# The last head of an attention kernel: score matmuls in pairs on both halves of the partitions, exponentials of 1024 columns

## The chip, the cores and the metric

One core of a Trainium2 chip runs the whole program. The metric is the device time of one execution in microseconds, as the median of several runs. Before the change it is 1465.34 us (three runs, 1463.74 to 1465.86).

## What is computed

Two sequences of 2048 tokens, width 256: 16-head attention with 16 columns a head and rotary positions, added to the input and normalised; then a gated feed-forward (token shift, sigmoid gate, squared relu key, value) over the same 4096 tokens, added and normalised.

```python
q, k, v = (heads(x @ W + b) for W, b in ((Wq, bq), (Wk, bk), (Wv, bv)))
q, k = rotary(q), rotary(k)
y = layernorm(x + softmax(q @ k.T / sqrt(16)) @ v)
xr = mu_r * y + (1 - mu_r) * y_prev          # y_prev: the token before
xk = mu_k * y + (1 - mu_k) * y_prev
r = sigmoid(xr @ W_r.T)
out = layernorm(y + r * (square(relu(xk @ W_k.T)) @ W_v.T))
```

## The kernel before, in words

The 32 heads (2 sequences x 16) run one after the other. `SEQ` is 2048, `TOK` 512, `P` 128; a head has `TILES` = 16 key tiles of 128 keys and `BLOCKS` = 4 blocks of 512 queries, so 64 items, numbered through all heads by `item(h, kt, j)`. `LAST` is head 31.

Queries and keys of a head lie as a stack of 48 rows (high and low parts, so that a product of rounded floats keeps its accuracy) in `q_stack` and `k_stack`. Two more query rows (against rows of ones in `k_stack`) carry the negative maximum of each query, so that a score matmul of 50 rows gives scores with the maximum already taken off. The stack of head h lies on partitions 0 to 63 if h is even, on 64 to 127 if it is odd (`stack_rows`), in one of two slots (`slot_of`). `load_neg` writes the two rows of maxima, by way of DRAM.

Per head and key tile (`period`, line 716) TensorE does: four score matmuls (line 733), each keys x 512 queries into one of three `score_ps` banks in turn; between them two maximum units for a later head (`maximum`, line 647), each two matmuls of 512 columns into one of two `ring_ps` buffers of two banks; and the value products of the tile before (`pv_half`, line 679), two times four matmuls of 256 columns, each on its own 32 columns of the array, adding into `pv_ps`. The maximum matmuls of a later head stand on the other 64 partitions than the scores: for its first `EARLY` = 8 units such a head reads a copy of its stack that `load_copy` has laid on the other side (512 queries and all the keys).

ScalarE turns every score bank into `probs` by an exponential of 512 columns (line 917). It waits for `scores_ready`, and at the start of a tile for `pv_done`, since `probs` holds two tiles. TensorE waits for `exps_done` before it writes a score bank again and before a value product. VectorE reads each ring buffer with a maximum over 1024 columns (line 1254); after a head it turns `pv_ps` over (`turn_context`), takes the inverse of the sums (`invert_sums`), and POOL scales the context and adds it to the input (`add_context`). TensorE's value products of the next head wait for `pv_turned`.

In the last head no maxima are left. TensorE fills their place with the gate products of the feed-forward's blocks 0 and 1 (`first_r`, `project_r`, line 697) in groups of four matmuls, into the ring buffers. VectorE does the second stage's preparation meanwhile: `before_tokens` and `mix` (the token shift) of block 0, then the context of head 30, then `before_tokens` and `mix` of block 1, then statistics (`tile_stats`), `normalise` and `flip_block` of blocks 2 and 3, whose turned tiles SP lays down by DMA (`land`, 16 DMAs a block), and `before_tokens`, `mix` of block 2. It then waits for the context of head 31.

After the last head TensorE goes through the eight blocks of the feed-forward: `project_key(0)`, then for each n the gate products of block n + 2, `value(n)`, `project_key(n + 1)`. The bank lists `key_ps`, `value_ps` and `r_ps` (ring 0, ring 1, ring 0, ...) say where they go. ScalarE takes the sigmoids of blocks 0 and 1 first, then the key of block 0 (`take_key`), and so on; it has to load another activation table between the exponentials and the sigmoids. Each engine's order is the program's order; the engines meet only at semaphores.

Of the kernel before, what the change touches and what calls it, by code (L numbers as in the profile page):

```python
# [53 lines left out]
EARLY = 2 * LEAD  # L54
COPY_Q = EARLY // 2 * P
FIRST_COPY = SIDES
TWINS = {0: (STACKS - 1, EARLY, MAX_UNITS), 1: (STACKS - 2, 0, EARLY)}
NEG_CYCLE = TILES - LEAD
NEG_LOADS = 1
CTX_BUFS = 2  # L60
R_AHEAD = 2
FLIPS = 4 * 4
POOL_BLOCKS = 2
RECIP_CYCLE = 4
# [98 lines left out]
def build(nc, x_tok, x_blk, w_first, w_qk, b_qk, w_v, b_v, w_rkv, mu, tables, out):  # L163
# [7 lines left out]
    with ExitStack() as ctx:  # L171
# [90 lines left out]
        y_blk = [y_half[:, n] for y_half in (y_first, y_second) for n in range(BLOCKS)]  # L262


        score_ps = [pb(f"score_ps{i}", [P, TOK]) for i in range(SCORE_BANKS)]
        ring_ps = [pb(f"ring_ps{i}", [P, 2 * TOK]) for i in range(2)]
        pv_ps = pb("pv_ps", [P, TOK])
        proj_ps = (*score_ps, pv_ps)
        ring_halves = [ring[:, c * TOK:(c + 1) * TOK] for ring in ring_ps for c in range(2)]
# [41 lines left out]
        copy_in = [sem(f"copy_in{i}") for i in range(SIDES)]  # L311
        ones_set = sem("ones_set")
        neg_in = [sem(f"neg_in{i}") for i in range(STACKS)]
        scores_ready = sem("scores_ready")
        exps_done = sem("exps_done")
        pv_done = sem("pv_done")
# [56 lines left out]
        def stack_rows(h, first, count):  # L373

            side = h % SIDES * SIDE_ROWS
            return slice(side + first, side + first + count)

        def slot_of(h):
            return h // SIDES % (STACKS // SIDES)
# [17 lines left out]
        def _(sp):  # L397
# [24 lines left out]
            def load_copy(h):  # L422

                slot, side, row = slot_of(h + 1), h // QUAD % 2, h % QUAD * HEAD_DIM
                q = cuts[row:row + HEAD_DIM, side, :, 0:COPY_Q]
                k = cuts[QUAD_ROWS + row:QUAD_ROWS + row + HEAD_DIM, side, :, :]
                first = 0
                for a, reps in BAND_GROUPS:
                    rows = stack_rows(h + 1, first * HEAD_DIM, reps * HEAD_DIM)
                    first += reps  # L430
                    sp.dma_start(q_stack[rows, slot, 0:COPY_Q].bitcast(F32), q[:, a:a + 1, :].broadcast_to([HEAD_DIM, reps, COPY_Q]))\
                        .then_inc(copy_in[h % SIDES], DMA)
                    sp.dma_start(k_stack[rows, slot, :].bitcast(F32), k[:, 0:reps, :]).then_inc(copy_in[h % SIDES], DMA)

# [22 lines left out]
            def load_neg(h):  # L457

                sp.wait_ge(neg_flipped, h + 1)
                sp.dma_start(neg_d[h % 2], neg_turned[:, h % 2]).then_inc(neg_out, DMA)  # L460
                sp.wait_ge(neg_out, (h + 1) * DMA)
                dst = q_stack[stack_rows(h, ROWS, PARTS), slot_of(h), :].bitcast(F32)
                sp.dma_start(dst.rearrange("a (t i q) -> a t i q", i=P // VCOLS, q=VCOLS),
                             neg_d[h % 2].rearrange("(i a t) q -> a t i q", i=P // VCOLS, a=PARTS))\
                    .then_inc(neg_in[h % STACKS], DMA)

            sp.dma_start(w_qk_s[:, :, 0:P], w_first).then_inc(w_first_in, DMA)
            for c, signal in enumerate((x_first_in, x_in[0])):
# [121 lines left out]
        def _(pe):  # L590
# [88 lines left out]
            def pv_half(h, kt, half):  # L679
# [8 lines left out]
                if half == 1:  # L688
                    mm.then_inc(pv_done, 1)

            def pv(h, kt):

                for half in range(2):
                    pv_half(h, kt, half)
# [15 lines left out]
                            mm.then_inc(r_ready, 1)  # L710
                        yield

            first_r = itertools.chain.from_iterable(project_r(n, VCOLS) for n in range(R_AHEAD))


            def period(h):

                k = RING_BASE[h]

                pe.wait_ge(neg_in[h % STACKS], neg_loaded(h))  # L720
                for kt, ops in enumerate(period_ops(h)):

                    work = ring_ops(ops, k)
                    k += ring_len(ops)
                    for j in range(BLOCKS):
                        n = item(h, kt, j)
                        rows, slot = stack_rows(h, 0, ROWS_M), slot_of(h)
                        queries = q_stack[rows, slot, :].rearrange("r (c j t) -> r j c t", j=BLOCKS, t=VCOLS)

                        if n < SCORE_BANKS:  # L730
                            pe.wait_ge(evacuated, LAST_IN_BANK[n] - BLOCKS + 1)
                        pe.wait_ge(exps_done, n + 1)
                        mm = pe.matmul(score_ps[n % SCORE_BANKS][:, :], k_stack[rows, slot, kt * P:(kt + 1) * P],  # L733
                                       queries[:, j], start=True, stop=True)
                        mm.then_inc(scores_ready, 1)
                        next(work, None)
                        if j % 2:
                            pv_before(h, kt, j // 2)
                            if h == LAST and kt > 0 and (j > 1 or kt == 1):
                                if (kt, j) == (1, 1):  # L740
                                    pe.wait_ge(ring_freed, RING_CREDIT + RING_TOTAL)
                                next(first_r, None)
                    for _ in work:
                        pass
                if h == LAST:
                    for _ in first_r:
                        pass

            def pv_before(h, kt, half):
# [34 lines left out]
                        next(terms)  # L784
                    done = due
            assert next(terms, None) is None
            for h in range(ALL_HEADS):
                if h == LAST:
                    pe.wait_ge(c_in, 2 * DMA)
                period(h)  # L790
            pv(LAST, TILES - 1)


            def value(n):
# [36 lines left out]
                    mm.then_inc(kv_ready, 1)  # L831

            project_key(0)
            for n in range(END - 2):
                for _ in project_r(n + R_AHEAD, P):
                    pass
                value(n)
                project_key(n + 1)
# [9 lines left out]
        def _(act):  # L848
# [60 lines left out]
            def period(h):  # L909
                for kt in range(TILES):  # L910
                    act.wait_ge(pv_done, h * TILES + kt + 1)
                    for j in range(BLOCKS):
                        if (h, kt, j) == (0, 0, 2):
                            take(len(WORK) - 1)
                        n = item(h, kt, j)
                        act.wait_ge(scores_ready, n + 1)
                        act.activation(probs[:, kt % 2, j, :], score_ps[n % SCORE_BANKS][:, :], ACT.Exp,  # L917
                                       scale=SCALE).then_inc(exps_done, 1)

            for h in range(ALL_HEADS):  # L920
                period(h)


            def take_turned(n):
# [40 lines left out]

            act.wait_ge(c_small, 1)
            act.wait_ge(ones_set, 2)
            for n in range(R_AHEAD):
                sigmoid(n)
            take_key(0)  # L970
            for n in range(A_GROUPS - 1):
                if BLOCKS <= n + R_AHEAD + 1 < A_GROUPS:
                    take_turned(n + R_AHEAD + 1)
# [188 lines left out]
        def _(dve):  # L1162
# [243 lines left out]
            edge(0)  # L1406
            before_tokens(0)
            mix(0)
            turn_context(LAST - 1)
            invert_sums(LAST - 1)  # L1410
            before_tokens(1)
            mix(1)
            tile_stats(range(POOL_BLOCKS * TPB, TILES))
            for n in range(POOL_BLOCKS, BLOCKS):
                normalise(n)
# [117 lines left out]
```

## Time and profile before

| | |
|---|---|
| median of three runs | 1465.34 us |
| profiled execution, its time | 1466.05 us |
| its span | 1464.2 us |
| TensorE busy, share of the span | 1443.7 us, 99% |
| VectorE busy | 1375.7 us, 94% |
| ScalarE busy | 1194.1 us, 82% |
| POOL busy | 307.0 us, 21% |
| first score of the last head | 1334.34 us |
| last value product of the last head ends | 1381.92 us |
| TensorE ends | 1456.2 us |

Times inside the execution count from the start of its span. Busy time of matmuls is modelled, since they are pipelined: two that overlap are each shown with their full length. The chain of waits is followed back from the last instruction, and gives each stretch of time to one piece of work. One float32 product of the program shows as two matmul records.

### The profile page before, as it was taken

How to read it: one execution, taken by the hardware profiler on the slowest of the kernel's cores; microseconds unless marked ns; L12 is line 12 of the kernel's file. 1: busy time of each engine (PE TensorE's matmuls, PEld its weight loads, DVE VectorE, ACT ScalarE, POOL GpSimd, SP SyncE). 2: the span in 40 equal slices, each digit the busy share in tenths (PEclk: the TensorE clock that was granted, in tenths of full speed). 3: DMA queues.
4: the chain of work that ended last, by engine and by line, in shares of the span. 5: the costliest groups of instructions: out<-in, count | busy, mean ns of one | idle time of the engine just before them, and what ended most of it. 6: DMA issues, size and time to landing. Idle time of an engine off the chain costs nothing.

```text
span 1464.2 us, 31722 instructions
## 1 busy us (share of the span) xinstructions
PE 1443.7 (99%) x13128; PEld 603.9 (41%) x13128; DVE 1375.7 (94%) x1459; ACT 1194.1 (82%) x2185; POOL 307.0 (21%) x277
## 2 busy tenths in 40 slices
PE   8999999999999999999999999999999999999998
PEld 6663333333333333333333333333333333333475
DVE  5779999999999999999999999999999999997396
ACT  4448888888888888888888888888888888888745
POOL 3430221032103210022103210331002000001175
PEclk9999999999999999999999999999999999999999
DMA  7755122232223221312223222322111323200153
GB/s 228 229 135 176 28 33 37 36 94 38 37 37 95 37 36 25 82 28 37 37 36 95 37 38 37 95 38 32 25 25 32 52 36 52 37 2 9 24 112 119
DMA packets 73056, 88.50 MB, mean 60 GB/s; under 512 B 48656, under 2 KB 58512, under 8 KB 66704
## 3 DMA queue, kind: packets, MB, share of 16 engines
q1 hardware_dynamic: 72352, 85.69, 27.9%
q8 instruction: 103, 1.69, 0.5%
q10 hardware_dynamic: 560, 0.79, 0.2%
q14 instruction: 41, 0.34, 0.1%
HBM read 29.50 MB, written 14.16 MB: 30 GB/s over the span
## 4 chain that ended last, share of the span: by engine, by line
PE 96%; ACT 1%; DMA 1%; DVE 1%; issue 0%; POOL 0%; POOLq 0%; ACTq 0%; DVEq 0%
PE pv_ps L685 40%; PE score_ps L733 33%; PE ring_ps L666 14%; PE score_ps L623 2%; PE ring_ps L705 2%; PE score_ps L818 2%; ACT probs L917 1%; PE score_ps L639 1%; PE pv_ps L623 1%; PE pv_ps L802 1%; PE score_ps L802 1%; DMA rope<-tables 1%; PE pv_ps L639 0%; PE ring_ps L818 0%; DMA w_raw<-w_first 0%
## 5 line engine op out<-in xcount | busy, mean ns | idle before, releaser
L1254 DVE TENSOR_REDUCE tile_max<-ring_ps 128x1 f32<-128x1024 f32 x1024 | 1232.7, 1217 | 33.7 <-PE ring_ps L666 25.5
L917 ACT ACTIVATE probs<-score_ps 128x512 f32<-128x512 f32 x2048 | 1107.7, 595 | 170.4 <-PE score_ps L733 129.9
L733 PE MATMUL score_ps<-q_stack,k_stack 50*128 50x512 f32 x2048 | 754.9, 448 | 7.1 <-ACT probs L917 6.9
L666 PE MATMUL ring_ps<-k_stack,q_stack 48*128 48x512 f32 x2048 | 733.3, 443 | 0.0
L685 PE MATMUL pv_ps<-probs,v_aug 128*32 128x256 f32 x8192 | 649.0, 391 | 0.0
L733 PEld LDWEIGHTS score_ps<-q_stack,k_stack 50*128 50x128 f32 x2048 | 304.4, 185 | 429.1 <-ACT probs L917 412.2
L685 PEld LDWEIGHTS pv_ps<-probs,v_aug 128*32 128x32 f32 x8192 | 166.0, 108 | 367.3 <-issue 190.0
L666 PEld LDWEIGHTS ring_ps<-k_stack,q_stack 48*128 48x128 f32 x2048 | 299.9, 184 | 7.0 <-DVE tile_max L1254 3.3
L1014 POOL TENSOR_TENSOR neg_cuts<-neg_max,zeros 128x16 fp32r<-128x16 f32 x31 | 6.8, 219 | 496.0 <-DVE neg_max L1227 496.0
L1006 POOL TENSOR_TENSOR v_aug<-v_all,b_v_s 128x256 f32<-128x256 f32 x32 | 23.5, 737 | 312.8 <-PE pv_ps L685 252.9
L1023 POOL TENSOR_TENSOR ctx_part<-ctx_turn,recip 128x256 f32<-128x256 f32 x32 | 20.1, 628 | 268.8 <-DVE recip L1281 268.8
L1035 POOL TENSOR_TENSOR rope<-rope 128x2048 f32<-128x2048 f32 x14 | 63.8, 4573 | 8.6 <-DMA rope<-qk_raw 8.6
L1276 DVE STREAM_TRANSPOSE ctx_turn<-pv_ps 128x512 f32<-128x512 f32 x32 | 22.6, 706 | 22.1 <-PE pv_ps L685 22.1
L868 ACT ACTIVATE probs<-score_ps,b_qk_s 128x512 f32<-128x512 f32 x21 | 14.4, 687 | 24.1 <-PE score_ps L623 24.1
L1041 POOL TENSOR_TENSOR rope<-rope 128x2048 f32<-128x2048 f32 x7 | 32.1, 4582 | 0.1
L1057 POOL TENSOR_TENSOR rope<-rope 128x2048 fp32r<-128x2048 f32 x7 | 32.0, 4570 | 0.1
L705 PE MATMUL ring_ps<-w_rkv_s,rope 128*32 128x256 f32 (+1 forms) x224 | 31.6, 379 | 0.0
L948 ACT ACTIVATE v_all<-score_ps 128x512 f32<-128x512 f32 x14 | 7.6, 594 | 22.7 <-PE score_ps L818 22.7
L705 PEld LDWEIGHTS ring_ps<-w_rkv_s,rope 128*32 128x32 f32 (+1 forms) x224 | 22.5, 144 | 7.3 <-issue 2.4
L818 PE MATMUL score_ps<-rope,w_rkv_s 128*128 128x512 f32 x56 | 25.3, 594 | 0.0
L1356 DVE SCALAR_TENSOR_TENSOR rope<-rope,mu_s 128x512 f32<-128x512 f32 x32 | 22.3, 756 | 2.1 <-ACT rope L929 2.1
L1028 POOL TENSOR_TENSOR z_s<-z_s,ctx_part 128x256 f32<-128x256 f32 x32 | 23.6, 738 | 2.5
(138 smaller groups left out, 546.4 us busy)
## 6 DMA issues: line engine op xcount, KB each, us to landing
k_stack<-rope SPq DMA_DIRECT2D x61, 256.0 KB, 5.2
k_stack<-rope SPq DMA_DIRECT2D x63, 128.0 KB, 4.8
q_stack<-rope SPq DMA_DIRECT2D x31, 256.0 KB, 4.4
qk_raw<-probs SPq DMA_DIRECT2D x28, 256.0 KB, 3.2
rope<-qk_raw SPq DMA_DIRECT2D x7, 1024.0 KB, 4.9
rope<-qk_raw SPq DMA_DIRECT2D x14, 512.0 KB, 6.4
q_stack<-rope SPq DMA_DIRECT2D x33, 128.0 KB, 4.9
z_s<-x_tok SPq DMA_DIRECT2D x2, 2048.0 KB, 12.5
```

The source lines that it names most:

```text
L623: mm = pe.matmul(bank, w[:, c, :], x[:, c, :], start=term == 0 and c == 0, stop=term == TERMS - 1 and c == CHUNKS - 1)
L666: mm = pe.matmul(ring_ps[k % 2][:, c * TOK:(c + 1) * TOK], q_stack[rows, slot, qt * P:(qt + 1) * P], k_stack[rows, slot, lo + c * TOK:lo + ...
L685: mm = pe.matmul(pv_ps[j * VCOLS:(j + 1) * VCOLS, t], v_aug[:, h % 2, kt, :], probs[:, kt % 2, j, t], start=kt == 0 and half == 0, stop=kt ...
L705: mm = pe.matmul(r_ps[n][g:g + width, q * DIM:(q + 1) * DIM], mixed[:, n % MIXED_BUFS, 0, c, q * P + g:q * P + g + width], w_rkv_s[:, 0, c ...
L733: mm = pe.matmul(score_ps[n % SCORE_BANKS][:, :], k_stack[rows, slot, kt * P:(kt + 1) * P], queries[:, j], start=True, stop=True)
L802: mm = pe.matmul(value_ps[q // 2][:, q % 2 * DIM:(q % 2 + 1) * DIM], key_act[:, n % 2, c, q * P:(q + 1) * P], w_rkv_s[:, 2, c, :], start=c ...
L818: mm = pe.matmul(o, w_rkv_s[:, 1, c, m * P:(m + 1) * P], mixed[:, n % MIXED_BUFS, 1, c, :], start=c == 0, stop=c == CHUNKS - 1)
L917: act.activation(probs[:, kt % 2, j, :], score_ps[n % SCORE_BANKS][:, :], ACT.Exp, scale=SCALE).then_inc(exps_done, 1)
L1035: pool.tensor_tensor(blocks, blocks, tables_s[:, :, w, :], ALU.mult).then_inc(quad_step, 1)
L1041: pool.tensor_tensor(raw, raw, swapped, ALU.add).then_inc(quad_step, 1)
L1057: pool.tensor_tensor(cuts[:, g % 2, 1, :].bitcast(F32R), raw, cuts[:, g % 2, 0, :], ALU.subtract)\
L1254: dve.reduce_max(tile_max[:, h % 2, unit // 2, unit % 2:unit % 2 + 1], slot[:, :], AX.X)\
```

## The change

For the last head alone:

- `load_copy(LAST)` copies all 2048 queries to the other 64 partitions (it was 512), and `load_neg(LAST)` writes the two rows of negative maxima a second time, there. So the whole stack of the last head lies on both sides.
- The three score banks become one tensor, and `wide_ps` names three slots of two banks: ring 0, score banks 0 and 1, ring 1.
- TensorE runs `last_period`: two pairs of score matmuls a tile, the two of a pair on the two sides and into the two banks of a slot; then the value products of the tile before in one piece (`pv_whole`, four matmuls of 512 columns). After tile 0's scores come the value products of head 30's last tile and the wait for `pv_turned`; before, that wait stood behind two scores of tile 1.
- ScalarE takes one exponential of 1024 columns for each pair.
- The gate products are no longer spread through the head. Two of block 0's eight groups stand ahead of the last value products, six behind them; those of block 1 follow `project_key(0)`, in the form of 128 columns. ScalarE takes the key of block 0 ahead of the sigmoid of block 1.
- VectorE does `before_tokens(1)` and `mix(1)` ahead of head 30's context, not behind it.

```diff
+WIDE = 2
+R_FILL = 2
-        score_ps = [pb(f"score_ps{i}", [P, TOK]) for i in range(SCORE_BANKS)]
+        scores = pb("scores", [P, SCORE_BANKS * TOK])
+        score_ps = [scores[:, i * TOK:(i + 1) * TOK] for i in range(SCORE_BANKS)]
         ring_ps = [pb(f"ring_ps{i}", [P, 2 * TOK]) for i in range(2)]
+        wide_ps = (ring_ps[0][:, :], scores[:, 0:WIDE * TOK], ring_ps[1][:, :])
...
-                q = cuts[row:row + HEAD_DIM, side, :, 0:COPY_Q]
+                queries = SEQ if h == LAST else COPY_Q
+                q = cuts[row:row + HEAD_DIM, side, :, 0:queries]
...
+                for place, signal in ((h, neg_in[h % STACKS]), (h + 1, neg_copy_in))[:1 + (h == LAST)]:
+                    dst = q_stack[stack_rows(place, ROWS, PARTS), slot_of(place), :].bitcast(F32)
+                    sp.dma_start(dst.rearrange("a (t i q) -> a t i q", i=P // VCOLS, q=VCOLS),
+                                 neg_d[h % 2].rearrange("(i a t) q -> a t i q", i=P // VCOLS, a=PARTS))\
+                        .then_inc(signal, DMA)
...
+            def pv_whole(h, kt):
+
+                for j in range(BLOCKS):
+                    pe.wait_ge(exps_done, SCORE_BANKS + item(h, kt, j // WIDE * WIDE) + WIDE)
+                    mm = pe.matmul(pv_ps[j * VCOLS:(j + 1) * VCOLS, :], v_aug[:, h % 2, kt, :], probs[:, kt % 2, j, :],
+                                   start=kt == 0, stop=kt == TILES - 1, skip_group_check=True)
+                mm.then_inc(pv_done, 1)
...
+            def last_period():
+
+                fill = project_r(0, VCOLS)
+                pe.wait_ge(neg_in[LAST % STACKS], neg_loaded(LAST))
+                pe.wait_ge(neg_copy_in, DMA)
+                pe.wait_ge(ring_freed, RING_CREDIT + RING_TOTAL)
+                for kt in range(TILES):
+                    for pair in range(WIDE):
+                        n = kt * WIDE + pair
+                        if n == 1:
+                            pe.wait_ge(exps_done, SCORE_BANKS + item(LAST, 0, 0))
+                        elif n >= len(wide_ps):
+                            pe.wait_ge(exps_done, SCORE_BANKS + item(LAST, 0, (n - len(wide_ps) + 1) * WIDE))
+                        for c in range(WIDE):
+                            rows, slot = stack_rows(LAST + c, 0, ROWS_M), slot_of(LAST + c)
+                            queries = q_stack[rows, slot, :].rearrange("r (c j t) -> r j c t", j=BLOCKS, t=VCOLS)
+                            mm = pe.matmul(wide_ps[n % len(wide_ps)][:, c * TOK:(c + 1) * TOK],
+                                           k_stack[rows, slot, kt * P:(kt + 1) * P], queries[:, pair * WIDE + c],
+                                           start=True, stop=True)
+                        mm.then_inc(scores_ready, WIDE)
+                    if kt == 0:
+                        pv(LAST - 1, TILES - 1)
+                        pe.wait_ge(v_aug_ready, LAST + 1)
+                        pe.wait_ge(pv_turned, LAST)
+                    else:
+                        pv_whole(LAST, kt - 1)
+                pe.wait_ge(exps_done, SCORE_BANKS + item(LAST, TILES - 1, 0))
+                for _ in range(R_FILL):
+                    next(fill)
+                pv_whole(LAST, TILES - 1)
+                for _ in fill:
+                    pass
...
-            for h in range(ALL_HEADS):
-                if h == LAST:
-                    pe.wait_ge(c_in, 2 * DMA)
+            for h in range(LAST):
                 period(h)
-            pv(LAST, TILES - 1)
+            pe.wait_ge(c_in, 2 * DMA)
+            last_period()
...
             project_key(0)
+            for n in range(1, R_AHEAD):
+                for _ in project_r(n, P):
+                    pass
...
+            for kt in range(TILES):
+                act.wait_ge(pv_done, LAST * TILES + kt + 1)
+                for pair in range(WIDE):
+                    n = kt * WIDE + pair
+                    act.wait_ge(scores_ready, item(LAST, 0, (n + 1) * WIDE))
+                    act.activation(probs[:, kt % 2, pair * WIDE:(pair + 1) * WIDE, :].rearrange("p j t -> p (j t)"),
+                                   wide_ps[n % len(wide_ps)], ACT.Exp, scale=SCALE).then_inc(exps_done, WIDE)
...
-            for n in range(R_AHEAD):
+            sigmoid(0)
+            take_key(0)
+            for n in range(1, R_AHEAD):
                 sigmoid(n)
-            take_key(0)
...
             mix(0)
+            before_tokens(1)
+            mix(1)
             turn_context(LAST - 1)
             invert_sums(LAST - 1)
-            before_tokens(1)
-            mix(1)
```

## Rows read from the trace of the kernel before

**Rows 1.** The page: span, and the granted TensorE clock in 40 slices

```profile
span 1464.2 us, 31722 instructions
...
PEclk9999999999999999999999999999999999999999
```

**Rows 2.** Chain that ended last, in the last head: start us, us, what

```profile
1343.23 0.67 PE score_ps L733 x2
1343.90 0.57 PE pv_ps L685 x8
...
1345.70 0.43 PE ring_ps L705 x8
```

**Rows 3.** Timeline of ScalarE, tile 0 to 1: start us, us, what [idle before]

```profile
1336.47 2.06 ACT L917 ACTIVATE probs<-score_ps 128x512 f32<-128x512 f32 x4 [0.52 <-PE score_ps L733]
```

**Rows 4.** Chain that ended last, behind the last head

```profile
1381.92 3.63 PE score_ps L818 x8
1385.55 3.45 PE ring_ps L705 x16
```

**Rows 5.** Stretch behind the last head: length, busy PE, PEld, DVE, ACT, POOL, PEclk, DMA, GB/s

```profile
1381.92:1456.20 74.28, 74.28 (x282) 53.39 (x282) 64.25 (x175) 41.34 (x71) 46.06 (x45) 1.00 0.38 99
```

**Rows 6.** An earlier head: timeline of TensorE (two rows), then its chain (one)

```profile
503.28 0.50 PE L733 MATMUL score_ps<-q_stack,k_stack 50*128 50x512 f32 x1
503.28 0.50 PE L666 MATMUL ring_ps<-k_stack,q_stack 48*128 48x512 f32 x1
...
505.01 0.23 PE ring_ps L666
```

**Rows 7.** Chain that ended last, where the last head begins

```profile
1334.34 0.67 PE score_ps L733 x2
1335.01 1.00 PE pv_ps L685 x16
1336.01 0.44 PE score_ps L733
...
1337.08 0.04 issue
```

**Rows 8.** Timeline of ScalarE: end of head 30, end of the last head

```profile
1332.39 2.26 ACT L917 ACTIVATE probs<-score_ps 128x512 f32<-128x512 f32 x4 [0.21 <-PE score_ps L733]
...
1380.84 1.28 ACT L935 ACT_TABLE_LOAD   x1
1382.13 1.94 ACT L935 ACTIVATE rope<-ring_ps 128x1024 f32<-128x1024 f32 x2
```

**Rows 9.** Groups of ScalarE by line and shape: busy us, mean ns of one

```profile
L917 ACT ACTIVATE probs<-score_ps 128x512 f32<-128x512 f32 x64 | 34.6, 596 | 11.5 <-PE score_ps L733 10.3
...
L935 ACT ACTIVATE rope<-ring_ps 128x1024 f32<-128x1024 f32 x7 | 7.0, 1011 | 1.3 <-PE ring_ps L705 1.3
```

**Rows 10.** Timeline of SP's DMA issues

```profile
1254.29 0.62 SPq L431 DMA_DIRECT2D q_stack<-rope  x1
...
1327.52 0.63 SPq L463 DMA_DIRECT2D q_stack<-neg_turned_rows  x1
1348.49 22.26 SPq L542 DMA_DIRECT2D rope<-rope  x32
```

**Rows 11.** Timeline of VectorE in the last head

```profile
1336.08 0.72 DVE L1276 STREAM_TRANSPOSE ctx_turn<-pv_ps 128x512 f32<-128x512 f32 x1 [5.41 <-PE pv_ps L685]
...
1337.00 2.43 DVE L1336 TENSOR_SCALAR rope<-rope,mu_c 128x511 f32<-128x511 f32 x4
1339.35 2.72 DVE L1356 SCALAR_TENSOR_TENSOR rope<-rope,mu_s 128x512 f32<-128x512 f32 x4
1342.11 0.17 DVE L1347 TENSOR_TENSOR rope<-mu_c,rope 128x4 f32<-128x4 f32 x1
...
1360.76 1.67 DVE L1336 TENSOR_SCALAR rope<-rope,mu_c 128x511 f32<-128x511 f32 x4 [9.58 <-DMA rope<-rope]
...
1381.96 0.72 DVE L1276 STREAM_TRANSPOSE ctx_turn<-pv_ps 128x512 f32<-128x512 f32 x1 [16.68 <-PE pv_ps L685]
```

**Rows 12.** Opening of the program: the stretch 22 to 24, and line 623 in it

```profile
22.00:24.00 2.00, 2.00 (x5) 1.53 (x5) 2.00 (x3) 0.39 (x1) 2.00 (x2) 0.50 0.60 90
...
L623 PE MATMUL pv_ps<-early_high,w_low x2: 628/628/628, 22.7 to 23.2; 128*128 128x512 f32 x2
```

More of the change, by code:

```diff
@@ L313, in build @@
         neg_in = [sem(f"neg_in{i}") for i in range(STACKS)]
+        neg_copy_in = sem("neg_copy_in")
         scores_ready = sem("scores_ready")
@@ L430, in load_copy @@
                     first += reps
-                    sp.dma_start(q_stack[rows, slot, 0:COPY_Q].bitcast(F32), q[:, a:a + 1, :].broadcast_to([HEAD_DIM, reps, COPY_Q]))\
+                    sp.dma_start(q_stack[rows, slot, 0:queries].bitcast(F32), q[:, a:a + 1, :].broadcast_to([HEAD_DIM, reps, queries]))\
                         .then_inc(copy_in[h % SIDES], DMA)
@@ L461, in load_neg @@
                 sp.wait_ge(neg_out, (h + 1) * DMA)
[L462 to L465, printed above, removed]
+                for place, signal in ((h, neg_in[h % STACKS]), (h + 1, neg_copy_in))[:1 + (h == LAST)]:
[3 more added lines that the diff above has]
+                        .then_inc(signal, DMA)
             sp.dma_start(w_qk_s[:, :, 0:P], w_first).then_inc(w_first_in, DMA)
@@ L711, in project_r @@
                         yield
-            first_r = itertools.chain.from_iterable(project_r(n, VCOLS) for n in range(R_AHEAD))
+            def last_period():
[29 more added lines that the diff above has]
+                    pass
             def period(h):
@@ L738, in period @@
                             pv_before(h, kt, j // 2)
[L739 to L742, printed above, removed]
                     for _ in work:
-                        pass
-                if h == LAST:
-                    for _ in first_r:
                         pass
@@ L786, in _ @@
             assert next(terms, None) is None
-            for h in range(ALL_HEADS):
-                if h == LAST:
-                    pe.wait_ge(c_in, 2 * DMA)
+            for h in range(LAST):
                 period(h)
-            pv(LAST, TILES - 1)
+            pe.wait_ge(c_in, 2 * DMA)
+            last_period()
             def value(n):
@@ L918, in period @@
                                        scale=SCALE).then_inc(exps_done, 1)
-            for h in range(ALL_HEADS):
+            for h in range(LAST):
                 period(h)
+            for kt in range(TILES):
[5 more added lines that the diff above has]
+                                   wide_ps[n % len(wide_ps)], ACT.Exp, scale=SCALE).then_inc(exps_done, WIDE)
             def take_turned(n):
```

## The prediction

> **What bounds the kernel now.** I read the page first: the chain that ended last is 96% TensorE, and the granted clock stands at its upper level (2.4 GHz) in all 40 slices [rows 1]. That alone doesn't tell what an edit of one head is worth, so next I read the chain inside the last head. One key tile there is two times a pair of score matmuls (0.67 us) and half a value product (0.57), and once a group of gate products (0.43): 2 x (0.67 + 0.57) + 0.43 = 2.91 us [rows 2]. TensorE has no gap in it. ScalarE needs only four exponentials per tile, one every 0.49 us where they stand back to back (2.06 = 3 x 0.487 + 0.60) [rows 3], and waits. So the last head is bound by TensorE, and from its end at 1381.92 TensorE runs without a gap to 1456.20 [rows 4, 5]. Whatever comes off the stretch from the first score of the last head (1334.34) to the second-stage gate product of block 2 (1385.55), 51.21 us, comes off the run, if the other engines follow. "x2" of a value or gate matmul in the records is one instruction of the program: float32 products show twice.
>
> **What a pair of sides is worth.** In earlier heads a score matmul and a maximum matmul, on different 64-partition sides, run at once: both 503.28 with 0.50 us [rows 6]. There four matmuls take 0.43 + 0.23 = 0.66 us of the chain. In the last head two on one side take the same 0.67 [rows 2]. So two score matmuls on two sides cost what one costs: 0.43 first after another kind of work, 0.23 as a follower (a third row of [rows 6]). Four scores of a tile, issued as two pairs, are 0.66 instead of 1.34. The value product in one piece: both halves back to back took 1.00 us (x16) [rows 7], so four products of 512 columns are put at 1.00, not 1.14. TensorE's work per tile becomes 0.66 + 1.00 = 1.66 us, and the gate groups leave the loop.
>
> **What ScalarE costs then.** Two exponentials of 1024 columns per tile. No exponential of that shape is in the trace. The nearest rows are the sigmoids, 128x1024 out of the same kind of bank: 1.01 us each, and two back to back 1.94 us, so one starts 0.92 us after the other [rows 8, 9]. By the same reading the 512 exponentials start every 0.49 at 0.60 long, the same overlap of about 0.1. The bounds of the pitch are 0.92 and 1.05 (no overlap, and the 0.04 us from an exponential's end to the next matmul that the chain has, 1337.08 [rows 7]). I take 0.93. ScalarE then needs 1.86 us per tile, more than TensorE's 1.66, and becomes the bound of the last head.
> The Trainium skill (ScalarE: Activation LUTs, What ACT_TABLE_LOAD costs) gives 186 ns + 0.833 ns a column and an overlap of about 93 ns; by it a 1024 exponential would start every 0.946 us, an estimate, and the sum would be 0.5 us longer. For 512 columns it says 612 ns where the trace has 596 [rows 9], so I stay with the rows.
>
> **Does the ring of three slots close in that time?** From the end of an odd exponential: its two value products 1.00, plus a first score pair 0.43, plus about 0.1 of signals = 1.53 us, when the exponential that needs them starts 1.86 - 0.10 = 1.76 later. 0.2 us to spare per tile; the second pair has 0.23 more and nearly a microsecond more time. TensorE waits on ScalarE, not the reverse, but narrowly.
>
> **Working of the new stretch**, from 1334.34:
> 1. Tile 0: two pairs 0.67, last value product of head 30 1.00, as now [rows 7]. The second pair and the product wait for head 30's exponentials, which end at 1332.39 + 2.26 = 1334.65 [rows 8]: hidden. The wait for the second copy of the negative maxima: the row write was issued at 1327.52 [rows 10], the new one 0.63 later, so 6 us stay until 1334.34; it costs nothing. The queue load of the copy grows from 512 to 2048 columns of queries, issued at 1254.29 [rows 10], 80 us ahead of the last head, and first used by the maxima of the last head, in the last key tiles of head 29; SP waits for nothing there. Nothing.
> 2. New order of waits: tile 1's first pair now stands behind VectorE's transposition of head 30's context, where before it stood ahead. The transposition took 0.72 us and started 0.07 after the product [rows 7, 11]. With 0.05 to signal, 0.84. Queued behind it on TensorE is everything; ScalarE has the two exponentials of tile 0 until then. What moved ahead of it on VectorE is the token shift and mix of block 1, 2.43 + 2.72 + 0.17 = 5.3 us, in an idle time of 5.41 [rows 11]: free, with 0.1 to spare. If that cover is gone, each 0.1 us costs 0.1 once.
> 3. First pair of tile 1, 0.45 with its signal. The third exponential starts at 1334.34 + 0.67 + 1.00 + 0.84 + 0.49 = 1337.34.
> 4. 29 further starts x 0.93 = 26.97: the last exponential starts at 1364.31, takes 1.01, ends 1365.32.
> 5. Last two value products after it: 1.04 -> 1366.36. Two of the eight gate groups of block 0 stand ahead, in TensorE's wait for that exponential.
> 6. Six gate groups at 0.43 = 2.58 -> 1368.94.
> 7. Key products of block 0, 3.63 as now [rows 4] -> 1372.57. Gate products of block 1, in the full-width form, 3.45 [rows 4] -> 1376.02. Then block 2's, which began at 1385.55.
> Gain 1385.55 - 1376.02 = 9.5 us. By the same steps: the loop gives 47.58 down to 32.02 = 15.6, and 6.0 of it goes back as gate work that the loop no longer carries. Against its own time the profiled execution (1466.05, span 1464.2) would go to 1456.5, span 1454.7. The median of the runs is 0.7 below the profiled one, so the forecast against the median is 1465.34 - 9.5 = 1455.8 us.
>
> **Do the others follow?** VectorE's next chain starts from the end of the head: 1381.96 becomes 1366.4, 15.6 earlier, while TensorE's consumers come 9.5 earlier, so all that hangs on it gains 6 us of room; POOL and late transposes hang on VectorE. The one thing on absolute time is the landing of blocks 2 and 3, 32 DMAs that SP issues in 22.26 us from 1348.49 [rows 10]; block 2 had landed at 1360.76 [rows 11], 12.3 after the first. Moving the mix of block 1 ahead brings the statistics and flips 5.2 earlier, so the DMAs start near 1343.3, and blocks land near 1355.6 and 1366.8. Block 2's is needed by 1376, block 3's by VectorE at about 1367.4. It fits with 0.6, and VectorE has 6 us behind it. ScalarE's table load of 1.28 [rows 8] ends near 1366.6, before block 0's gate is ready at 1368.9.
>
> **Rivals.**
> - *Exponentials don't overlap at this width* (pitch 1.05): 29 x 0.12 = 3.5 us less gain, 1459.3. Against it: two sigmoids of that size did [rows 8]. 7 in 100.
> - *The ring of waits is the bound.* If the last two value products can't run beside the first two but only behind them, 0.85 us follow 0.85 us, the loop grows by about 0.5 to some 2.3 us a tile, 14.5 x 0.43 = 6.2 us are lost, 1462.0. The 0.2 us of room in the loop makes it possible; that four column groups run at once in 0.57 [rows 2] speaks against it. 8 in 100.
> - *The pairs don't overlap* (the change doesn't do what it says): TensorE 2.1 us a tile, 3.6 lost, 1459.4. [rows 6] speaks against it. 2 in 100.
> - *A late landing or VectorE gives part of it back*: VectorE is busy 64.25 of 74.28 us after the head [rows 5]. DMAs ten microseconds later would eat its 6 us of room and 4 more: 1460. 4 in 100.
> - *Slower: the clock falls in the last head.* TensorE would for the first time pause in each tile (about 0.2 of 1.86 us, in one or two pieces). At the lower level (1.2 GHz, granted 0.50) matmuls of 512 columns started 0.43 apart in a stretch that followed 3 us of near idleness [rows 12], against 0.23 at the upper. A tile would be 2 x 1.66 = 3.3 us, the stretch 14.5 x 1.46 = 21 us longer, 1477. It decides from a mean tile of 1.86 + 9.5/14.5 = 2.5 us, that is with some 45% of the tiles at the lower level. Against it: no stretch with pauses this short is seen with a lower clock. 5 in 100.
> The Trainium skill (TensorE: Matmul & The Clock Gate, A second HAM failure mode: psum-queue depth-cycling) describes such a case, pauses between groups of matmuls that cycle through banks with the clock swinging; by that rule the run would end near 1477. The trace has no such pauses in a head, so it can't say.
>
> **How the numbers follow.** Forecast 1455.8 with 74 in 100. Its own range is 1454.3 (pitch 0.92, full overlap of fills) to 1457.5. The range given is 1454.3 to 1462.0: it takes in the pitch's upper bound, the failed pairs, late landings and the edge of the wait-bound case, and leaves out the clock and a tail at either end. About 0.2% (2.9 us) is what a measurement can tell from no change, so faster means below 1462.4. Faster 0.90 (the forecast, most rivals and three quarters of the wait-bound case), same 0.04, slower 0.06 (the clock and unknown things).
>
> **What would show it.** Exponentials of 1024 columns starting 0.92 to 0.95 apart from about 1337.3, with no idle time of ScalarE between them; paired score matmuls with equal starts; TensorE busy some 90% from 1337 to 1365 at a granted clock of 1.00; head end near 1366.4; block 2's gate products near 1376.0; no gap on TensorE after it. The forecast is wrong if ScalarE waits for scores in each tile, if the clock row falls, or if TensorE waits for VectorE or a landing behind the head.

## The result and the profile after

| | before | after |
|---|---|---|
| median of the runs beside each other | 1464.54 us (4 runs, 1463.29 to 1465.86) | 1454.01 us (4 runs, 1453.75 to 1454.18) |
| ratio, 95% interval | | 0.993 (0.9915 to 0.9945) |
| profiled execution, its span | 1466.05, 1464.2 | 1454.18, 1452.1 |
| first score of the last head | 1334.34 | 1331.74 |
| key products of block 0 begin | 1381.92 | 1366.47 |
| first value product of block 0 begins | 1389.01 | 1377.01 |
| from the first score to that value product, "the stretch" | 54.67 us | 45.27 us |
| from there to the end of the span | 75.2 us | 75.1 us |

Faster by 0.7%, as forecast, but the time lies 0.3 us under the low end of the range. The last three lines say where to look. The stretch, forecast to lose 9.5 us, lost 9.40. What follows it is the same. Yet the spans differ by 12.1 us: the last head began 2.6 us earlier, before anything of the change had run. One of the six runs of one_side below, 1486.61 us at a mean clock of 0.979, stands in a slower state than all others and is left out there.

The chain of the changed kernel where the last head begins, and in its loop (start us, us, what; line 744 is the paired scores, 702 the value products in one piece):

```profile
1331.74 0.43 PE ring_ps L744 x2
1332.18 0.44 PE scores L744 x2
1332.62 1.04 PE pv_ps L692 x16
1333.66 0.02 issue
1333.68 0.73 DVE ctx_turn L1324
1334.41 0.14 issue
1334.55 0.74 PE ring_ps L744 x4
...
1345.55 0.67 PE ring_ps L744 x4
1346.22 1.16 PE pv_ps L702 x8
1347.38 0.43 PE scores L744 x2
1347.81 0.24 PE ring_ps L744 x2
1348.05 1.16 PE pv_ps L702 x8
...
1362.05 0.86 PE ring_ps L720 x16
1362.91 0.89 PE pv_ps L702 x7
1363.80 2.67 PE ring_ps L720 x47
1366.47 3.63 PE scores L855 x8
1370.10 6.91 PE ring_ps L720 x32
```

Against [rows 2]: four scores of a tile now take 0.43 + 0.23, where they took two times 0.67, the gate groups (line 720) are gone from the loop, and a tile takes 0.67 + 1.16 = 1.83 us where it took 2.90. The value products show 1.16 and not 1.00: the wait for ScalarE stands inside them (half_exp below takes that wait away, and they show 0.99).

ScalarE in the same time:

```profile
1332.30 1.02 ACT L967 ACTIVATE probs<-ring_ps 128x1024 f32<-128x1024 f32 x1 [0.24 <-PE ring_ps L744]
1333.22 1.02 ACT L967 ACTIVATE probs<-scores 128x1024 f32<-128x1024 f32 x1
1335.17 1.94 ACT L967 ACTIVATE probs<-ring_ps 128x1024 f32<-128x1024 f32 x2 [0.93 <-PE ring_ps L744]
...
1346.11 2.00 ACT L967 ACTIVATE probs<-ring_ps 128x1024 f32<-128x1024 f32 x2
1347.94 1.08 ACT L967 ACTIVATE probs<-scores 128x1024 f32<-128x1024 f32 x1
1348.86 2.00 ACT L967 ACTIVATE probs<-ring_ps 128x1024 f32<-128x1024 f32 x2
...
1361.69 1.08 ACT L967 ACTIVATE probs<-scores 128x1024 f32<-128x1024 f32 x1
1366.58 1.28 ACT L982 ACT_TABLE_LOAD   x1 [3.81 <-PE ring_ps L720]
```

From 1335.17 to the end of its last exponential, 1362.77, ScalarE has no idle time: three exponentials every 2.75 us, 0.917 from start to start. Before, it waited 0.52 us at the tile of [rows 3], and 11.5 us over the head [rows 9]. The one gap, 0.93 us at 1335.17, is the wait for head 30's context. The second row that moved is the landing on VectorE:

```profile
1333.68 0.72 DVE L1324 STREAM_TRANSPOSE ctx_turn<-pv_ps 128x512 f32<-128x512 f32 x1 [1.18 <-PE pv_ps L692]
...
1352.63 1.67 DVE L1384 TENSOR_SCALAR rope<-rope,mu_c 128x511 f32<-128x511 f32 x4 [9.09 <-DMA rope<-rope]
...
1363.93 0.72 DVE L1324 STREAM_TRANSPOSE ctx_turn<-pv_ps 128x512 f32<-128x512 f32 x1 [6.78 <-PE pv_ps L702]
```

From the head's first score block 2's landing came at 20.9 us, where in [rows 11] it came at 26.4.

### The profile page after: what moved, and what is told of

It is laid out like the page before. It is cut to its first block, busy times and chain, and to the rows that moved or that the text cites. A ratio compares the mean times of both kernels' runs of the same rounds, so it can differ in the third digit from the quotient of the medians.

```text
span 1452.1 us, 31356 instructions
## 1 busy us (share of the span) xinstructions
PE 1432.9 (99%) x12952; PEld 600.0 (41%) x12952; DVE 1375.0 (95%) x1459; ACT 1188.2 (82%) x2153; POOL 305.6 (21%) x277
## 4 chain that ended last, share of the span: by engine, by line
PE 96%; ACT 1%; DVE 1%; DMA 1%; issue 0%; POOL 0%; POOLq 0%; ACTq 0%; DVEq 0%
PE pv_ps L692 39%; PE scores L778 31%; PE ring_ps L673 14%; PE scores L630 2%; PE ring_ps L720 2%; PE scores L855 2%; ACT probs L957 1%; PE pv_ps L702 1%; PE scores L646 1%; PE pv_ps L630 1%; PE scores L839 1%; PE pv_ps L839 1%; DMA rope<-tables 1%; PE ring_ps L744 0%; PE pv_ps L646 0%; PE scores L744 0%
## 5 line engine op out<-in xcount | busy, mean ns | idle before, releaser
L957 ACT ACTIVATE probs<-scores 128x512 f32<-128x512 f32 x1984 | 1073.0, 595 | 158.9 <-PE scores L778 119.6
L778 PE MATMUL scores<-q_stack,k_stack 50*128 50x512 f32 x1984 | 731.4, 448 | 6.9 <-ACT probs L957 6.7
L692 PE MATMUL pv_ps<-probs,v_aug 128*32 128x256 f32 x7936 | 628.7, 391 | 0.0
L778 PEld LDWEIGHTS scores<-q_stack,k_stack 50*128 50x128 f32 x1984 | 294.9, 185 | 415.6 <-ACT probs L957 399.1
L692 PEld LDWEIGHTS pv_ps<-probs,v_aug 128*32 128x32 f32 x7936 | 160.6, 108 | 355.8 <-issue 179.2
L908 ACT ACTIVATE probs<-scores,b_qk_s 128x512 f32<-128x512 f32 x21 | 14.4, 687 | 24.0 <-PE scores L630 23.2
L995 ACT ACTIVATE v_all<-scores 128x512 f32<-128x512 f32 x14 | 7.6, 595 | 28.1 <-PE scores L855 28.1
L720 PE MATMUL ring_ps<-w_rkv_s,rope 128*128 128x256 f32 (+1 forms) x176 | 29.4, 379 | 0.0
L720 PEld LDWEIGHTS ring_ps<-w_rkv_s,rope 128*128 128x128 f32 (+1 forms) x176 | 24.5, 161 | 6.2 <-issue 2.6
L855 PE MATMUL scores<-rope,w_rkv_s 128*128 128x512 f32 x56 | 25.3, 594 | 0.0
```

The costliest lines, as they stand in the source:

```text
L692: mm = pe.matmul(pv_ps[j * VCOLS:(j + 1) * VCOLS, t], v_aug[:, h % 2, kt, :], probs[:, kt % 2, j, t], start=kt == 0 and half == 0, stop=kt ...
L720: mm = pe.matmul(r_ps[n][g:g + width, q * DIM:(q + 1) * DIM], mixed[:, n % MIXED_BUFS, 0, c, q * P + g:q * P + g + width], w_rkv_s[:, 0, c ...
L855: mm = pe.matmul(o, w_rkv_s[:, 1, c, m * P:(m + 1) * P], mixed[:, n % MIXED_BUFS, 1, c, :], start=c == 0, stop=c == CHUNKS - 1)
```

## The experiments

The measure in most of them is the stretch, from the last head's first score to block 0's first value product. It repeats to the hundredth of a microsecond: 45.27 in after, again and after_warm, 54.67 in before, before_warm and before_warm2. The time of a run also holds the opening, which scatters, so both are given.

### Where do the other 2.6 us come from?

The transposition of a head's context on VectorE comes 2.6 us earlier in the profile of after, for the first head (140.95 against 143.54) as for the thirtieth (1293.88 against 1296.48). So the difference arises ahead of the first head. There the granted clock differs (columns: length; busy PE, PEld, DVE, ACT, POOL; granted clock; DMA share; GB/s). Before, in which the idle 3.1 us of TensorE at 18.6 to 21.7 are followed by the lower clock ([rows 12] is the second row of these):

```profile
20.00:22.00 2.00, 0.29 (x1) 0.29 (x2) 2.00 (x4) 1.45 (x3) 0.74 (x1) 0.67 0.00 0
...
24.00:26.00 2.00, 2.00 (x10) 1.89 (x9) 1.90 (x4) 0.04 (x1) 0.58 (x1) 0.50 0.99 189
26.00:28.00 2.00, 2.00 (x13) 2.00 (x13) 1.90 (x4) 1.18 (x2) 0.00 (x0) 0.62 0.85 313
```

After, where the same wait was 2.4 us long and ended at the same time, 21.67 against 21.71:

```profile
20.00:22.00 2.00, 0.33 (x1) 0.30 (x2) 2.00 (x4) 1.49 (x3) 0.78 (x1) 1.00 0.00 0
22.00:24.00 2.00, 2.00 (x14) 1.77 (x13) 2.00 (x3) 0.35 (x1) 2.00 (x2) 1.00 0.61 90
24.00:26.00 2.00, 2.00 (x20) 2.00 (x19) 1.90 (x4) 0.05 (x1) 0.57 (x1) 1.00 0.84 160
```

Is that chance, or does the change move the opening? **again** is the changed kernel unaltered.

> The changed kernel unaltered, in more runs. Theory A (the stretch of the last head gained what was forecast, 9.4 us; the other 2.6 us between the two profiled executions is the opening of the program, where the clock fell in the execution of before and not in that of after, by chance): the runs of before fall into two groups some 2.6 us apart, near 1463.5 and 1466, with granted clocks of 1.00 and under; the changed kernel has both groups too, 1454.0 and 1456.6, if its opening is open to the same chance. Theory B (the change itself moves the opening): the changed kernel never shows the upper group, and its gain to the lower group of before is 9.4, to the upper 12.

1455.15 us (5 runs, 1452.64 to 1456.17), ratio 0.9938 (0.9926 to 0.9951). The kernel before in the same session: 1464.3 us, 17 runs from 1461.77 to 1465.84. Not two groups but a spread of some 4 us, in both kernels. The profiles of six variants of the changed kernel, with the same opening, show the lower clock in it too (the table below). So theory B falls: the changed kernel has slow openings as well. Theory A's two groups were too simple.

**before_warm** puts dummy matmuls into the idle time of the opening, in the kernel before; **before_warm2** is the same again, beside **after_warm**, the changed kernel with them.

```diff
             for n in FIRST_ORDER:
+                if n == 3:
+                    for _ in range(6):
+                        for g in range(0, P, VCOLS):
+                            pe.matmul(pv_ps[g:g + VCOLS, :], warm[:, 0:VCOLS], warm, start=True, stop=True)
                 project(n)
```

> The kernel before with six groups of four dummy matmuls (zeros, into the value bank that the next projection overwrites) in TensorE's idle time of the opening, 18.5 to 21.7 us. Nothing else differs. Theory A: the clock doesn't fall there, and all runs are near the faster ones of before, 1463.4 (at most 0.3 more, if the dummies run over the end of the idle time). If the clock of the opening has nothing to do with the scatter: the runs scatter over 1463.3 to 1465.9 as before.

1463.38 us (11 runs, 1462.55 to 1463.95), where the kernel before had 1464.3. The forecast holds.

> The kernel before with the same dummy matmuls, again, beside after_warm on the same chip: about 1463.4, some 1 us under the kernel before, whose runs go up to 1465.8 where the clock falls in the opening.

1463.47 us (11 runs, 1462.64 to 1464.59), where the kernel before had 1464.06 (15 runs, 1462.21 to 1465.53).

> The changed kernel with the dummy matmuls in the opening's idle time. With the same opening on both sides the difference to before_warm2 is the change alone. If the 9.4 us of the stretch are all of it: 9.4 us under before_warm2, about 1454.0, runs within 1.5 us of each other. If the change also does something to the opening: more than 10.5 under it.

1454.08 us (5 runs, 1452.84 to 1455.94). The medians differ by 1463.47 - 1454.08 = 9.4 us, what the stretch says. The runs are not within 1.5 us of each other but within 3.1; the longest, 1455.94 us, has a mean clock of 0.996.

All profiled executions together. The second column is the mean granted clock of the first 40 us, the third the end of that idle time, when VectorE delivers the low parts of a block of the input (`x_split`):

| | clock, 0 to 40 us | the wait ends, us | last head starts, us | difference |
|---|---|---|---|---|
| before | 0.91 | 21.71 | 1334.34 | 1312.63 |
| exp512 | 0.91 | 20.30 | 1333.18 | 1312.88 |
| no_fill | 0.91 | 21.53 | 1333.14 | 1311.61 |
| old_order | 0.96 | 21.39 | 1333.04 | 1311.65 |
| late_wait | 0.96 | 21.47 | 1332.94 | 1311.47 |
| one_side | 0.96 | 20.71 | 1332.37 | 1311.66 |
| half_pv | 0.96 | 20.19 | 1331.76 | 1311.57 |
| after | 1.00 | 21.67 | 1331.74 | 1310.07 |
| again | 1.00 | 19.92 | 1330.12 | 1310.20 |
| half_exp | 1.00 | 21.70 | 1331.84 | 1310.14 |
| before_warm | 1.00 | 21.97 | 1332.11 | 1310.14 |
| before_warm2 | 1.00 | 21.81 | 1331.85 | 1310.04 |
| after_warm | 1.00 | 21.25 | 1331.34 | 1310.09 |
| best | 1.00 | 21.43 | 1331.58 | 1310.15 |

The last column separates two causes. At full clock the last head starts 1310.04 to 1310.20 us after the end of the wait, in seven of seven executions; where the clock fell, 1.3 to 2.8 us later than that. And the end of the wait itself lies anywhere from 19.92 to 21.97 us. Followed back along the chain, it hangs on VectorE's work and this on a landing by DMA: the tables for the rotation landed at 11.45 us in again and at 13.44 in before. For the two executions of the result the waits ended together, so nearly all of their 2.6 us is the clock.

Of ten executions without the dummies seven had the lower clock in the opening, of four with them none, with 1.75 to 1.92 us of the idle time left. The length of the wait alone does not decide. These two kept the full clock (again, then half_exp), while no_fill lost it after 2.49 us:

```profile
19.92 0.73 PE L630 MATMUL pv_ps<-early_high,w_high 128*128 128x512 f32 x2 [3.29 <-DVE x_split L1244]
21.70 0.73 PE L630 MATMUL pv_ps<-early_high,w_high 128*128 128x512 f32 x2 [3.09 <-DVE x_split L1244]
```

What decides stays open. The runs that were not profiled have a mean clock for the whole run only. Among the profiled ones it is 0.997 or 0.998 where the opening was slow and 0.999 or 1.000 where it was not. Of the kernel before, 31 of 41 runs have 0.998 or less, with a median of 1464.5 us, and the other ten have 1463.3. With the dummies it is 8 of 22, 1463.5, and the others 1463.4. So the clock still falls somewhere in some runs with the dummies, but it costs next to nothing there. By their medians alone the dummies are not proven: the ratios to the kernel before are 0.9995 (0.9986 to 1.0003) and 0.9998 (0.9989 to 1.0007). The spread of the kernel before is narrower with them, 1462.55 to 1464.59 in 22 runs against 1461.77 to 1465.84 in 41; that of after_warm is not.

### Do the two sides make the pairs short?

**one_side** puts both matmuls of a pair on the last head's own side.

```diff
-                            rows, slot = stack_rows(LAST + c, 0, ROWS_M), slot_of(LAST + c)
+                            rows, slot = stack_rows(LAST, 0, ROWS_M), slot_of(LAST)
```

> The changed kernel with both score matmuls of a pair on the last head's own side. Theory A (pairs on two sides overlap and that is what makes the loop short): a tile costs TensorE 4 x 0.23 + 0.2 + 1.0 = 2.1 us, against 1.83 measured, the loop grows by 15 x 0.28 = 4 us: 1458. If ScalarE bounded it so loosely that the sides don't matter: 1454.

1460.06 us (5 runs, 1457.95 to 1460.22), ratio 0.9971 (0.9959 to 0.9982); the stretch 50.01, 4.74 more, where the forecast was 4 and a run of 1458. Its chain:

```profile
1358.98 0.67 PE ring_ps L744 x2
1359.65 0.47 PE scores L744 x2
1360.12 0.99 PE pv_ps L702 x8
1361.12 1.14 PE ring_ps L744 x4
1362.26 0.99 PE pv_ps L702 x8
```

A pair costs 0.47 as a follower where it cost 0.23, a tile 1.14 + 0.99 = 2.13 us, and the value products are down to 0.99: TensorE is the bound here and waits for nothing. With the rest of the change in place, the second side is worth 4.74 us of the 9.40.

### Who bounds the loop?

In the changed kernel both engines look full. **half_exp** takes work from ScalarE alone: only the first 512 columns of each slot are exponentiated, so half of the last head's probabilities are an older head's.

```diff
-                    act.activation(probs[:, kt % 2, pair * WIDE:(pair + 1) * WIDE, :].rearrange("p j t -> p (j t)"),
-                                   wide_ps[n % len(wide_ps)], ACT.Exp, scale=SCALE).then_inc(exps_done, WIDE)
+                    act.activation(probs[:, kt % 2, pair * WIDE, :], wide_ps[n % len(wide_ps)][:, 0:TOK],
+                                   ACT.Exp, scale=SCALE).then_inc(exps_done, WIDE)
```

> The changed kernel with ScalarE's exponentials of the last head cut to the first 512 of every 1024 columns (the other half of the probabilities is left as an older tile had it); signals and waits unchanged. Measured over the stretch from the last head's first scores to block 0's first value product, 45.27 us in the changed kernel. Theory A (ScalarE is the bound of the last head, TensorE could do a tile in 0.67 + 1.00): a tile falls from 1.83 to 1.67 us, the stretch by 14.5 x 0.165 = 2.4, to 42.9, and value products take 1.00 us of the chain in place of 1.16. Theory B (the ring of waits or TensorE is the bound): the stretch stays within 0.5 us.

The stretch fell to 42.73 us (forecast 42.9; one run, 1451.75). Chain, then ScalarE:

```profile
1340.39 0.99 PE pv_ps L702 x8
1341.38 0.43 PE scores L744 x2
1341.82 0.23 PE ring_ps L744 x2
1342.05 0.99 PE pv_ps L702 x8
```

```profile
1338.61 0.60 ACT L967 ACTIVATE probs<-ring_ps 128x512 f32<-128x512 f32 x1 [0.58 <-PE ring_ps L744]
```

TensorE's own tile is 0.67 + 0.99 = 1.66 us, the forecast's number, and ScalarE bounds the changed kernel at 1.83. The ring of three slots holds neither back: here TensorE has no gap, and in after ScalarE has none.

**exp512** keeps all columns but takes them in exponentials of 512, two to a pair.

> The changed kernel with two exponentials of 512 columns in place of each of 1024. If ScalarE is the bound, a tile costs 4 x 0.487 = 1.95 us in place of 1.83, the stretch grows by 14.5 x 0.12 = 1.7 us to 47.0, and the run to about 1455.9. If TensorE or the ring is the bound, the finer signals help or change nothing: 45.3 or less.

1456.49 us (4 runs, 1455.24 to 1458.48), ratio 0.9948 (0.9934 to 0.9962); the stretch 47.14, 1.87 more. Its value products show 1.29 in the chain where after has 1.16:

```profile
1346.31 1.29 PE pv_ps L702 x8
```

The wider form of the exponential is worth 1.9 us, through ScalarE.

**half_pv** has the value products of all but the last tile in two halves (`pv(LAST, kt - 1)` in place of `pv_whole(LAST, kt - 1)`).

> The changed kernel with the value products of the last head in two halves of 256 columns (as in all other heads; the last tile's stay whole). Two halves back to back cost TensorE 1.00 us in head 30, a whole in the run with halved exponentials 0.99. Theory (ScalarE bounds the loop, halves cost TensorE nothing): stretch 45.3. Rival: the second half of the first two blocks stands behind the wait for the second pair's exponential, so TensorE loses the 0.16 us a tile that it has and more, and the stretch grows by 1 to 6 us.

The stretch 45.27 us (one run, 1454.22), the same to the hundredth: on TensorE's side of a loop that ScalarE bounds, "whole values" are worth nothing here. What the halves cost TensorE the run can't say: with 0.16 us to spare in a tile, a cost of up to that much would not show, and the chain has 1.16 or 1.17 for them, with the wait inside.

### The start and the end of the head

**late_wait** moves TensorE's waits for head 30's context behind tile 1's scores.

```diff
                         pv(LAST - 1, TILES - 1)
-                        pe.wait_ge(v_aug_ready, LAST + 1)
-                        pe.wait_ge(pv_turned, LAST)
                     else:
+                        if kt == 1:
+                            pe.wait_ge(v_aug_ready, LAST + 1)
+                            pe.wait_ge(pv_turned, LAST)
                         pv_whole(LAST, kt - 1)
```

> The changed kernel with TensorE's two waits (for head 30's context and the new values) moved behind the scores of tile 1, ahead of the first value product of the last head. In the profile of after, ScalarE stood idle 0.93 us at that place. Theory (term 2 of the sum, measured larger than forecast, is a wait that the scores needn't share): the third exponential starts 1.0 us earlier, and all that follows: 1453.0. Rival (the ring of waits passes the delay on to the fourth pair, which stands behind the same product): under 0.3 us gain.

The stretch 44.39, 0.88 less, where the theory had 1.0; 1454.13 us by the median of five runs (1452.85 to 1454.55) against 1455.15 of again on the same chip, within the scatter of the opening, so the stretch is the evidence. ScalarE there:

```profile
1334.41 1.02 ACT L968 ACTIVATE probs<-scores 128x1024 f32<-128x1024 f32 x1
1335.37 1.94 ACT L968 ACTIVATE probs<-ring_ps 128x1024 f32<-128x1024 f32 x2
```

The gap of 0.93 is gone. The first value product still waits 0.22 us for the context, and a little of it comes back.

**no_fill** (`R_FILL = 0`) leaves no gate groups ahead of the last value products.

> The changed kernel with none of block 0's gate groups ahead of the last value products (two stand there in the changed kernel). TensorE has about 0.7 us there from the end of the products before to the last exponential. The two groups cost 0.86 us: the stretch of 45.27 grows by 0.7 to 46.0. If they were not hidden: by nothing.

The stretch 46.14 us (one run, 1456.52), 0.87 more: both groups were hidden entirely.

**old_order** undoes VectorE's part: `before_tokens(1)` and `mix(1)` behind head 30's context.

```diff
-            before_tokens(1)
-            mix(1)
             turn_context(LAST - 1)
             invert_sums(LAST - 1)
+            before_tokens(1)
+            mix(1)
```

> The changed kernel with VectorE's token shift and mix of block 1 behind head 30's context again. Their 5.3 us then delay statistics, flips and landings of blocks 2 and 3 by 5.3. Block 2's landing would come at about 26.2 us from the head's first scores in place of 20.9, block 3's at 37 in place of 31.7; VectorE wants block 3 at 33.1. So VectorE would wait some 4 us there, of the 6 that it has in hand: the stretch stays 45.27, the run within 0.3 us of the changed kernel. Rival: the delay reaches TensorE, 1 to 4 us.

The stretch 45.27 us; 1455.48 us (4 runs, 1455.09 to 1456.09). From the head's first score block 2's landing came at 27.97 us (forecast 26.2), block 3's at 37.74 (forecast 37). VectorE:

```profile
1361.01 1.67 DVE L1384 TENSOR_SCALAR rope<-rope,mu_c 128x511 f32<-128x511 f32 x4 [10.92 <-DMA rope<-rope]
...
1370.78 1.67 DVE L1384 TENSOR_SCALAR rope<-rope,mu_c 128x511 f32<-128x511 f32 x4 [4.32 <-DMA rope<-rope]
```

It waits 4.32 us for block 3's landing, and none of it reaches TensorE. That part of the change buys room on VectorE, not time.

**best** has the later waits and the dummy matmuls.

> The changed kernel with the later wait of late_wait (0.88 us off the stretch there, 44.39) and the dummy matmuls in the opening's idle time of before_warm. Stretch 44.4. The median should be 1453.2 or less, and the runs should lie within some 1.5 us of each other, as with before_warm, in place of 3.5 (again).

1453.23 us (5 runs, 1452.82 to 1453.66), ratio 0.9924 (0.9912 to 0.9937); the stretch 44.39. Of the kernels that compute the whole result it has the lowest median, 0.85 us under after_warm (in another session), and the stretch is 0.88 shorter. Its runs lie within 0.84 us of each other; but those of after, without the dummies, lay within 0.43, so five runs show nothing about the spread.

## Why the prediction was right and where it was wrong

**The sum was right, in part by luck.** By its steps, from the last head's first score, in us:

| step | forecast | measured |
|---|---|---|
| 1 to 3: to the start of the third exponential | 3.00 | 3.43 |
| 4: 29 further starts | 26.97 (0.93 each) | 26.52 (0.914 each) |
| 4, 5: last exponential and last value products | 2.05 | 2.11 |
| 6: six gate groups | 2.58 | 2.67 |
| 7: key products, gate products of block 1 | 7.08 | 7.09 |
| sum | 41.68 | 41.82 |

Step 1 to 3 was 0.43 short. The largest part is an overlap that step 1 called hidden: the second pair of tile 0 starts only when head 30's exponentials have ended (at 1332.06), and costs 0.44 and not 0.23. The product took 1.04 for 1.00, from there to the release of TensorE it was 0.89 for 0.84 (the signal alone 0.14 for 0.05), and the first pair of tile 1 with its signal 0.62 for 0.49. Step 4 gave as much back, and nothing ties the two errors together: I had taken 0.93, a little above the sigmoids' 0.92 [rows 8], and the exponential starts every 0.917, or 0.914 over the whole row. By the Trainium skill's formula (ScalarE: Activation LUTs, What ACT_TABLE_LOAD costs) my estimate was 0.946, which would have made the sum 0.5 us longer. The trace does not agree: 29 starts at 0.914 are 0.9 us less than that.

**The bound of the loop** was named rightly: ScalarE at 1.83 us a tile (forecast 1.86), TensorE able to do 1.66 (half_exp). Of the rivals, exponentials without overlap (pitch 1.05) and the ring of waits are excluded by 0.917 and by half_exp; that the pairs don't overlap, by their 0.23 as a follower against 0.47 in one_side; a late landing, by the chain of after, in which TensorE has no gap behind the head. old_order used 4.3 us of the room on VectorE that was forecast as 6, and still none of it reached TensorE. The clock stood at 1.00 through the whole last head: waits of 0.16 us inside a tile brought no fall.

**One term had the right size, but its cause is not shown.** The value product in one piece was counted as 1.00 for 1.14 in TensorE's tile, and half_exp shows 0.99. Whether the one piece does it, or that no scores stand between the halves, no run separates: half_pv hides the difference behind ScalarE. In [rows 7] both halves of head 30's last product took 1.00 together, which speaks for the second.

**The failed step is the last one, from the sum to the time and its range.** I said that the profiled execution stands 0.7 us over the median, and took the median of three runs, 1465.34, as a fixed point. It isn't: over the sessions the same kernel ran from 1461.77 to 1465.86, with medians of 1464.1 to 1464.6. The miss of 1.8 us is made of two parts. The median before was 1464.54 when four runs were taken, 0.8 lower than my fixed point. The medians then differ by 10.5 us where the sum has 9.5 and the stretch 9.4; the other 1.1 us is the opening, since nothing else differs. The sum had taken it as the same on both sides. And a cause stood in my own rows: [rows 12] show the clock at 0.50 in the opening. I used it as a price for a rival, and not as what it was, a loss of some 2.5 us that the profiled execution of before had and another execution need not have (1.3 to 2.8 us or nothing, in the table above). The four runs of after were lucky: three of them have a mean clock of 0.999 or 1.000, against ten of 41 for the kernel before. The low end, 1454.3, took in the fastest exponentials, which are worth 0.3 us, and "full overlap of fills", for which I had no working, but no scatter of the opening. From a median of 1464.3 the same 9.5 us would have given 1454.8, and a range of 2 us to either side for the opening would have held both 1454.01 and again's 1455.15.

## What to carry to other kernels

Add up a change inside one stage from the rows of that stage, and check the result over that stage: here it repeats to 0.01 us while whole runs scatter by 4. Before giving a range, look where the executions of the unchanged kernel differ; a lower granted clock, or a wait for a landing, in a stretch that the change doesn't touch is a term of the range. Where two engines both look full, take work from one of them alone: half_exp told ScalarE's bound from TensorE's in one run.

## What the runs showed of the hardware

- Two matmuls of 50 rows and 512 columns (rounded floats) on the two 64-partition sides take 0.23 us together as a follower, two on one side 0.47 (after, one_side). The first after value products costs 0.2 us more in either case (0.43, 0.67).
- Exponentials of 1024 columns from two banks start every 0.917 us, a tile's four of 512 take 1.96 where its two wide ones take 1.83: the wide form saves about 0.06 us a pair, and 1.87 us over the head's 32 pairs.
- The load of another activation table did not run in ScalarE's idle time: in after ScalarE stood idle 3.81 us and loaded at 1366.58, when block 0's gate products were there; late_wait has the same (loaded at 1366.90, after 3.81 us). In the kernel the wait for these products stands ahead of the sigmoid, and the load seems to stand behind the wait. In [rows 8] the products were there already and the load ran at once. The prediction had the load end near 1366.6, in the idle time; it ended at 1367.86, and TensorE lost nothing by it.
- In ten executions TensorE stood idle for 2.41 to 3.31 us within 17 to 22 us of the start. In seven of them (2.49 to 3.31 us) a granted clock of 0.50 followed, which cost 1.3 to 2.8 us; three (2.41, 3.09 and 3.29) kept 1.00. In no_fill the clock was 0.50 at 11.6 to 14 us as well, after another wait of 2.23 us, which the dummies do not fill.
- With six groups of dummy matmuls in that idle time the granted clock of the opening was 1.00 in four of four profiled executions.
